# A recommendation tower on one core: first dense layer on two tiles at once, 36 cross terms for 40, an eleventh field by one-hot rows

## The reference

```python
e = jnp.stack([tbl_f[ids[:, f]] for f in range(26)], axis=1)      # 2048 x 26 x 32, tables of 1000 to 125000 rows
x1 = einsum('bik,bjk,hij->bhk', e, e, W1) + b1[None, :, None]     # 128 outputs
x2 = einsum('bik,bjk,hij->bhk', x1, e, W2) + b2[None, :, None]    # 128 outputs
z = jnp.sum(jnp.concatenate([x1, x2], axis=1), axis=-1)           # 2048 x 256
h = jnp.concatenate([z, dense_ctx], axis=1)                       # 2048 x 272
h = jnp.maximum(h @ W_top1 + b_top1, 0.0)                         # 512
h = jnp.maximum(h @ W_top2 + b_top2, 0.0)                         # 256
y = h @ W_top3
```

## Time and profile before

| | us |
|---|---|
| median of 3 runs | 509.12 |
| lowest, highest | 507.92, 512.33 |
| the profiled execution's own time | 510.54 |
| its span, first to last instruction | 508.7 |

### The profile page before, as it was taken

The page is one execution under the profiler, slowest core; times in us unless marked ns, Lnnn a source line. Parts: engine busy times, 40 slices in busy tenths (PEclk is TensorE's granted clock), DMA queues, the critical chain, the costliest instruction groups (busy, mean ns, idle before and its releaser), DMA issues.

```text
span 508.7 us, 25085 instructions
## 1 busy us (share of the span) xinstructions
PE 479.8 (94%) x10786; PEld 461.8 (91%) x10786; DVE 377.7 (74%) x1095; ACT 253.5 (50%) x530; POOL 348.9 (69%) x274
## 2 busy tenths in 40 slices
PE   4998889969699999999999999999999999999998
PEld 4887879869699999999999999999999999999997
DVE  8698949495778788797969597959695968773202
ACT  8866835364525463636364545454454545455111
POOL 5888977467887888787878787878787887700000
PEclk9999999989989999999999999999999999999999
DMA  6620022120111102020202020202020200000000
GB/s 216 171 95 13 15 56 47 28 60 13 37 40 30 44 16 53 13 59 10 59 12 58 13 58 13 57 13 59 11 59 12 59 10 12 9 1 3 1 1 1
DMA packets 14001, 19.57 MB, mean 38 GB/s; under 512 B 5123, under 2 KB 11528, under 8 KB 13838
## 3 DMA queue, kind: packets, MB, share of 16 engines
q0 software_dynamic: 8512, 4.38, 8.1%
q1 hardware_dynamic: 5454, 14.73, 8.0%
HBM read 19.08 MB, written 0.01 MB: 38 GB/s over the span
## 4 chain that ended last, share of the span: by engine, by line
PE 78%; DVE 8%; issue 3%; ACT 3%; DMA 3%; POOL 2%; SPq 1%; ACTq 0%; DVEq 0%; POOLq 0%
PE psum L927 21%; PE psum L901 18%; PE psum L946 12%; PE psum L972 8%; PE psum L880 7%; PE psum L994 4%; PE psum L922 4%; DVE work L631 3%; POOL emb L389 2%; DMA onehot<-in_tbl 2%; PE psum L967 2%; DVE onehot L479 2%; DMA emb<-in_tbl,idx 1%; ACT t_area L742 1%; ACT v L706 1%
## 5 line engine op out<-in xcount | busy, mean ns | idle before, releaser
L389 POOL DMA_INDIRECT emb<-in_tbl,idx x266 | 348.1, 1309 | 95.0 <-issue 63.5
L742 ACT COPY t_area<-psum 128x432 f32<-128x432 f32 x256 | 124.5, 543 | 98.2 <-PE psum L901 71.3
L631 DVE TENSOR_TENSOR work<-embT 128x32 f32<-128x32 f32 (+12 forms) x416 | 129.3, 386 | 0.0
L927 PE MATMUL psum<-t_area,v 128*128 (+1 forms) x1088 | 124.1, 275 | 0.0
L927 PEld LDWEIGHTS psum<-t_area,v 128*128 128x128 f32 x1088 | 122.8, 192 | 0.0
L901 PE MATMUL psum<-diag,work 64*64 64x54 f32 (+1 forms) x6144 | 102.1, 216 | 4.8 <-ACT t_area L742 2.0
L901 PEld LDWEIGHTS psum<-diag,work 64*64 64x64 f32 (+1 forms) x6144 | 93.3, 126 | 11.5 <-issue 6.0
L719 ACT COPY diag<-embT 32x416 f32<-32x416 f32 x128 | 69.9, 546 | 20.6 <-DVE embT L613 19.1
L946 PE MATMUL psum<-table_parts,onehot 125*128 125x96 bf16 x1350 | 63.7, 208 | 4.1 <-DVE onehot L479 2.4
L946 PEld LDWEIGHTS psum<-table_parts,onehot 125*128 125x128 bf16 x1350 | 59.4, 99 | 6.5 <-DVE onehot L479 2.7
L880 PE MATMUL psum<-diag,work 128*64 128x108 f32 (+1 forms) x1024 | 51.5, 262 | 8.5 <-DVE work L631 6.6
(11 more groups left out here) (96 smaller groups left out, 447.1 us busy)
## 6 DMA issues: line engine op xcount, KB each, us to landing
ids_all<-in_short_ids SPq DMA_DIRECT2D x15, 625.0 KB
emb<-in_tbl,idx POOLq DMA_INDIRECT x266
t_area<-in_L_rec_W SPq DMA_DIRECT2D x1, 1664.0 KB, 8.5
work<-in_W_top SPq DMA_DIRECT2D x2, 512.0 KB, 12.2
onehot<-in_tbl SPq DMA_DIRECT2D x5, 156.2 KB
onehot<-in_tbl SPq DMA_DIRECT2D x5, 125.0 KB
t_area<-in_L_rec_W SPq DMA_DIRECT2D x1, 338.0 KB, 4.0
idx<-in_ids SPq DMA_DIRECT2D x1, 208.0 KB, 2.5
```

The lines of the kernel that those rows point to most:

```text
L389: eng.indirect_dma_start(emb[n][:, f * K:(f + 1) * K], None, tables[f], bass.IndirectOffsetOnAxis(ap=idx[:, t * F + f:t * F + f + 1], axis=0),
L631: last = nc.vector.tensor_tensor(pairs[:, half, :, :, tri(r):tri(r) + r + 1], halves[:, g, :, 0:r + 1], halves[:, g, :, r:r + 1].broadcast ...
L742: nc.scalar.copy(dst, src).then_inc(t_out, 1)
L927: last = nc.tensor.matmul(z_ps(t)[:, NP:2 * NP], v[:, s, :], moments(slot), start=(a == 0), stop=(a == len(terms) - 1))
```

## The change

1. Layer 1 runs once for two tiles (a pair), with 256 columns in place of 128. It no longer stands inside a step. After every second step PE runs layer 2 of both tiles of the older pair and then layer 1 of the next pair (`layers`). The pair's hidden values take two PSUM banks, 4 and 7, and `h1_low` and `make_y` are done for two tiles at once, in every second tile of DVE.
2. The cross layer has 36 terms: 5 for x1 and 31 for x2. For this `pack` moves other pieces, in 10 copies where it had 7, with one wait of DVE for its own earlier copies.
3. 11 fields come by one-hot rows, in three parts of 4, 4 and 3 fields, before phases 1, 3 and 5. They take 38, 36 and 26 matmuls. Their PSUM banks are 7, 6 and 4. Parts 0 and 2 wait for `h1_low` of the pair, since they write where layer 1 wrote. So 15 gathers a tile remain.
4. The marks and the load of W_top3 move with this.

```diff
-FREE, U_Z2 = 5, U + 5
+FREE, U_Z2 = 8, U + 8
-U_Z1, N_Z1 = U + HF, 4
+U_Z1, N_Z1 = U + HF, 3
-SHORTS = 10
+SHORTS = 11
-PER_BANK = 5
+PER_BANK = 4
-MARK_PHASES = (0, 2, 3, 5, 6, 7)
+MARK_PHASES = (0, 2, 4, 6, 7)
...
         def rows_ps(part):
-            return psum[:, 7 - part, 0:PER_BANK * PARTS * K]
+            return psum[:, (7, 6, 4)[part], 0:PER_BANK * PARTS * K]
...
+        def h1_ps(half):
+            return psum[:, (4, 7)[half], :].rearrange("p (a b) -> p a b", b=2 * NP)
...
-                if not known or t >= 4:
-                    make_y(t - 4)
+                if n == 1 and (not known or t >= 5):
+                    for tile_of_pair in range(2):
+                        make_y(2 * i - 4 + tile_of_pair, tile_of_pair)
                 if not known or t >= 2:
                     pack(t - 1, 1 - n)
-                if not known or t >= 3:
-                    h1_low(t - 3)
+                if n == 1 and (not known or t >= 3):
+                    h1_low(i - 1)
...
-                        for part, at in enumerate((5, 6) if isinstance(t, int) and t == 1 else (2, 5)):
+                        for part, at in enumerate((5, 6, 7) if isinstance(t, int) and t == 1 else (1, 3, 5)):
...
-                    if part == 1 and not (isinstance(t, int) and t < 5):
-                        eng.wait_ge(y_ready, t - 3)
+                    if pair is not None:
+                        eng.wait_ge(y_ready if part == 1 else h1_lo_ready, 2 * pair + (1 if part == 1 else 3))
...
+            def layer1(pair):
+                if not (isinstance(pair, int) and pair == TILES // 2 - 1):
+                    eng.wait_ge(rows_ready, 2 * pair + 3)
+                eng.wait_ge(h1_lo_ready, 2 * pair + 1)
+                eng.wait_ge(z_out, 2 * pair + 2)
...
+                    if a == 2:
+                        eng.wait_ge(y_ready, 2 * pair + 1)
...
+                        if a == 0 and z is z_lo:
+                            eng.wait_ge(z_lo_ready, 2 * pair + 2)
...
+            def step(t, pair, n):
+                for half in range(2):
+                    t_units(t, half, pair)
+                if not isinstance(t, int) or t >= 2:
+                    cin(t - 1, n)
+            def layers(pair):
+                for n in range(2):
+                    layer2(2 * pair + n, pair, n)
+                layer1(pair + 1)
...
+            layer1(0)
             with eng.Fori(0, (LOOP[1] - LOOP[0]) // 2) as i:
                 with eng.Fori(0, 2) as n:
-                    step(2 * i + n + LOOP[0], n)
+                    step(2 * i + n + LOOP[0], i, n)
+                layers(i)
```

More of the change, by code:

```diff
@@ L298, in build @@
                 moves = [(0, hi - lo, 0, LOW, LOW * c, V_LOW + HF * (1 - c) + lo)]
[L299 to L303, removed]
+                for first, end, quadrant, _, slot in OTHERS[c]:
+                    a, z = max(lo, first), min(hi, end)
+                    if a < z:
+                        moves.append((a - lo, z - a, LOW, CONST + 1, 32 * quadrant, slot + a - first))
                 v_jobs.append(([("other", c, nu, CONST + 1) for nu in range(lo, hi)], moves))
@@ L323, in marks_in @@
         def marks_in(t):
-            layers, cross = t >= 3, t != 1
-            return len(MARK_PHASES) + 2 + 2 * layers + len(MARK_TERMS) * cross
+            layer1, layer2, cross = t >= 2 and t % 2 == 0, t >= 4 and t % 2 == 0, t != 1
+            return len(MARK_PHASES) + len(ROW_PARTS) + 2 * layer1 + 2 * layer2 + len(MARK_TERMS) * cross
         block = ctx.enter_context(nc.Block())
@@ L751, in z_move, with h1_move @@
                     .then_inc(z_out, 1)
[L753 to L759, removed]
+            def h1_move(pair):
+                if not (isinstance(pair, int) and pair < 1):
+                    eng.wait_ge(h2_full, 2 * pair)
+                for half in range(2):
+                    eng.wait_ge(h1_full, 2 * pair + half + 1)
+                    nc.scalar.activation(h1_hi[:, 2 * half:2 * half + 2, :], h1_ps(half), ACT.Relu).then_inc(h1_out, 1)
             def step(t, i, n):
@@ L777, in step @@
                 if not known or t >= 1:
-                    z_move(t - 1, 1 - n)
+                    z_move(t - 1, i - 1 + n, 1 - n)
+                if n == 0 and (not known or t >= 2):
+                    h1_move(i - 1)
             eng.wait_ge(consts_ready, 1)
@@ L792, in _ @@
                 step(t, t // 2, t % 2)
[L793 to L796, removed]
+            z_move(TILES - 1, TILES // 2 - 1, 1)
+            h1_move(TILES // 2 - 1)
         @block.tensor
@@ L848, in make_v, with t_units @@
                     last.then_inc(prep_full, 1)
-            def t_units(t, half):
+            def t_units(t, half, pair):
                 eng.wait_ge(pairs_ready, 2 * t + half + 1)
@@ L931, in cin, with short_rows @@
                 last.then_inc(z_full, 1)
-            def short_rows(t, part):
+            def short_rows(t, part, pair):
                 eng.wait_ge(onehot_ready, t)
@@ L964, in layer1 @@
                 for a in range(N1 // NP):
-                    dst = h1_ps(t)[:, a, :]
+                    if a == 2:
+                        eng.wait_ge(y_ready, 2 * pair + 1)
+                    dst = h1_ps(a // 2)[:, a % 2, :]
                     cols = slice(a * NP, (a + 1) * NP)
-                    nc.tensor.matmul(dst, top1d[:, cols], denseT[:, bass.ts(t, NP)], start=True, stop=False)
+                    nc.tensor.matmul(dst, top1d[:, cols], denseT[:, bass.ts(pair, 2 * NP)], start=True, stop=False)
@@ L993, in layer2 @@
                     for s in range(N1 // NP):
-                        last = nc.tensor.matmul(dst, h1[:, s * NP:(s + 1) * NP], top2[:, s, :], start=False,
-                                                stop=(h1 is lo and s == N1 // NP - 1))
-                        if h1 is lo and s == N1 // NP - 2:
+                        last = nc.tensor.matmul(dst, h1[:, s, n * NP:(n + 1) * NP], top2[:, s, :], start=False,
+                                                stop=(h1 is h1_lo and s == N1 // NP - 1))
@@ L997, in layer2 @@
+                        if h1 is h1_lo and s == N1 // NP - 2:
                             last.then_inc(progress, 1)
                 last.then_inc(h2_full, 1)
-            def step(t, n):
-                known = isinstance(t, int)
-                t_units(t, 0)
-                if not known or t >= 3:
-                    layer1(t - 3, n)
-                t_units(t, 1)
-                if not known or t >= 3:
-                    layer2(t - 3)
-                if not known or t >= 2:
+            def step(t, pair, n):
+                for half in range(2):
+                    t_units(t, half, pair)
+                if not isinstance(t, int) or t >= 2:
```

137 lines of the change are left out of this document (60 added, 77 removed).

## The result

| | us |
|---|---|
| median after (542.29 to 546.06) | 543.11 |
| median before, same chip (507.92 to 512.87) | 510.73 |
| after / before | 1.0648, 95% interval 1.0573 to 1.0723 |
| the profiled execution's own time; its span | 546.06; 544.1 |

The change makes the kernel 6.5% slower. The forecast was 530.0, range 515 to 540: right in sign and in what the loss comes from, a circle through DVE and the gathers, 13 too low, and 3 outside its range. The profiled execution is 3 over the median, where the forecast had allowed 1.4.

The account below looks back on a forecast made before the run. PE bounds the kernel before, a two-step circle through DVE after. A pair: 55.45 + 1.9 gathers + 0.3 clock = 57.65; five pairs +24.7, start +2.6, tail -6.4, total +20.9: 530.0 for the median, range 515 to 540.

Parts of the forecast that it names:

- a circle over two steps: PE's part 0 waits for DVE's `h1_low`, DVE's next tile for PE: 55.45 a pair, before 52.7.
- The pieces of the circle behind the transpose: DVE's work up to `h1_low`, done 24.45 after even R, with pack 4.0; then part 0 to next R, 8.75.
- The late gathers: DVE's second transpose of the odd tile waits for POOL's last gather, 0.3 to 3.4 late; 1.9 a pair taken.
- The long gather: On POOL, a gather beginning well inside DVE's pairs lasts until they end: 3.43 and 4.06 for 0.94.
- The clock: Half clock on PE after its waits, mostly falling into layer 1: 0.3 a pair, between 0 and 1.7.
- The start: R (end of a step's short rows) of step 4 at 182.1 for 179.5: +2.6, within 3 either way.
- Where PE waits: PE waits 5 us from even R, part inside layer 1 for `z_low`, the rest before part 0.
- The tail: After R of step 14 no one-hot is left on DVE, so PE's work decides: -6.4.
- Rival 1: On POOL, no late gathers: a pair is 55.75 and the time 520.5; chance 0.24.
- Rival 2: On PE, the half clock hits the short rows in each pair: +1.4 x 5, 537; chance 0.12.
- Rival 3: PE stays the bound and part 0 doesn't wait: ten steps 243.5, time 483; chance 0.06.

Follow-up runs that it names:

- ahead2: The changed kernel with the gathers' marks moved four marks earlier (AHEAD 2 for 6), nothing else: 512.48 us, 1.001 of before.
- h1_first: The changed kernel with `h1_low` moved ahead of the pack in DVE's odd tiles, nothing else: 542.07 us, 1.061 of before.
- swap_banks: The changed kernel with short-row parts 0 and 1 trading PSUM banks, so part 0 waits for `make_y` alone: 540.86 us, 1.060 of before.
- z_early: The changed kernel with `z_low` and `make_y` ahead of the second pairs in odd tiles, `h1_low` still last: 546.18 us, 1.070 of before.
- all_four: The changed kernel with `h1_low` before the pack, `z_low` and `make_y` early, AHEAD 2, parts before phases 3, 4, 5: 484.91 us, 0.950 of before.

## Why the prediction was right in kind and too low

- **The bound moves from PE to a circle over two steps: right.** Even step to odd step takes 37.1 in the mean for 35.4; odd to even 22.5 for 22.25.
- **The pieces of the circle behind the transpose: right.** From its start to `z_low` done it takes 15.0 to 15.5 (329.66 - 314.63), from there to `h1_low` done 6.0 to 6.7, from part 0 to R 9.0 for 8.75. The pack took 3.5 to 3.7 in odd tiles and 4.1 in even ones, for 4.0. Layer 1 at full clock takes 3.32 for 28 matmuls in the after trace (499.75 to 503.07), 0.119 each: 256 columns cost what 128 do, as the trace before had it.
- **The late gathers: this step failed in size.** "I take 1.9, the middle" over R + 2.9 makes R + 4.8 for the second transpose. It began at R + 7.77, 6.73, 6.85, 6.80 and 4.29, in the mean 6.5. The missing 1.7, five times, is 8.4 of the 10.0 that the ten steps took more (298.2 for 288.2). In the stretch shown the miss is three parts: the first gather began at R + 2.4 and not 1.6; both long gathers occurred, 5.7 in place of the middle's 4.5, and so in four of five pairs; slightly long ones came to 1.25 for 0.8. Together 2.45, the 26.86 at which the last began less the middle of 22.9 to 25.9. It even lies past the upper end (25.9). The middle between two patterns was no pattern at all. The fifth pair, with one long gather in that stretch, came out at 35.0. What the prediction took for granted here, that POOL cannot start the 15 before the stretch, is the marks' doing: ahead2 takes it away, a pair is 5.3 shorter and the kernel 30.6 faster. That is more than the 3.6 of lateness in the mean, since both transposes also start earlier than R + 2.9.
- **The long gather: read too simply.** "One that begins well inside the pairs lasts until they end" holds for some gathers only. In the trace before, two gathers begin 1.27 after the start of a run of pairs; one (185.37) takes 3.88, the other (212.43) 1.12. After the change two begin 1.63 after it and take 3.51 (291.51) and 1.04 (411.01). Even the same gather, the 60th of the program, is held in one execution and not in another. The first row is the changed kernel, 1.83 after the start of a run of pairs; the second is h1_first, whose list is the same up to there, 1.85 after it:

```profile
105.59 3.31 POOL L394 DMA_INDIRECT emb<-in_tbl,idx  x1 [0.30 <-issue]
```

```profile
105.04 1.20 POOL L394 DMA_INDIRECT emb<-in_tbl,idx  x1 [0.30 <-issue]
```

  What decides is not known, so the count of one or two long ones was what had been seen, and no rule. The Trainium skill was also read too simply there: the same section (SBUF — State Buffer, Who interferes with whom) says that a `tensor_tensor` with both inputs in SBUF contends with what GpSimd reads from SBUF. The pairs have both inputs in SBUF, and the list `idx` of the gathers lies there too. No run here tells whether that read is what is held.
- **The clock: near.** Layer 1 after `z_low` takes 4.6 to 5.3 at the 1.2 GHz level. In the loop most of it lies beside make_y and the pack; DVE waits 3.4 in five pairs for the hidden values, 0.7 a pair for the 0.3 taken. In the first pair less lies beside it: PE waits 7.97 until 146.47, the second `h1_low` waits 1.50 for the hidden values, and is done at 153.10 where I had 151 (159.9 less 8.75).
- **The start: past its bound in this execution.** R of step 4 is 186.7 for 182.1, 4.6 later where I had allowed 3. Of the 4.6 about 2.0 is the late `h1_low`, 2.0 lies between it and R of step 3, where PE has gaps of 0.57 and 0.90, and 0.6 in the step behind. Not all of it belongs to the kernel. h1_first and swap_banks run the same order up to `z_low` of the first pair, and in their profiles the second transpose ahead of it waits 2.5 and 2.3 for its gather, where it waits 5.9 in the changed kernel. Why it does is not shown. `z_low` comes 2.35 and 1.8 earlier and R of step 4 is 183.7 and 183.5, inside the bound.
- **Where PE waits: wrong.** The forecast put 5 "part of it inside layer 1 for `z_low` ..., the rest before part 0". Measured, 6.2 a pair inside layer 1 and under 0.4 before part 0. I had `z_low` due at R + 18 without the late gathers, and layer 1 at full clock behind it. In the pair shown `z_low` is done at R + 21.9 (329.66), and layer 1 then takes 4.6, so that PE comes to part 0 just before `h1_low` is ready. The way from the transpose to `h1_low` lasts no longer than I had summed, but the wait stands elsewhere. For the sum it makes little difference, for a remedy a great deal: h1_first and swap_banks mend the place named in the forecast and give next to nothing.
- **The tail: right**, 59.2 after R of step 14 for 59.3.
- **The rivals.** Rival 1 (no late gathers) is the reverse of what happened. The Trainium skill (SBUF — State Buffer, Who interferes with whom) was on its side: by it a `tensor_tensor` leaves descriptor generation alone. The trace after disagrees again for the two that took 3.51 and 4.10, where most take 0.94. Rival 2 (half clock on the short rows) didn't happen: part 0 took 1.79 each time. Its mechanism is real, as z_early shows, where the wait stands directly ahead of the rows; here layer 1 took the blow. Rival 3 (PE stays the bound) is what all_four reaches, by another order of the same work.
- **The range** ended at 540, which is 530.0 with both terms at their upper ends (1.5 x 5 for the gathers, 3 for the start). In the profiled execution both went past these: 3.6 for the gathers in the mean over 3.4 (25.9 less 22.6 is 3.3, in fact), 4.6 for the start over 3. Its time is 14.7 over the 531.4 forecast for it: 10.0 from the ten steps, 4.6 from the start. The bound on the gathers was no bound, since it took the first gather's start as known.

What stays open: how the rest of the 4.6 before step 4 divides between clock and gaps; what makes one gather long and another short; and what the merged layer 1 or the eleventh field cost or give each by itself, since no run has one without the other.

## What to carry to other kernels

Where a change makes PE wait on a helper engine, write the circle: each piece from the moment PE frees it to the moment PE needs it again, the DMA issue queue included; if one stretch of it becomes shorter than that queue's work, the queue is part of the circle, and both its long cases should be counted, not their middle. Two waits in a row on the same engine can stand in for one another: here taking away either gave nothing (540.9, 546.2), both together 29. And a change that loses 6% as written was a gain of 5% with three calls moved, gathers freed earlier and two parts of the short rows put later, so find the wait that took its place before the change is dropped.

## What was not expected of the hardware

- A gather that begins inside a run of `TENSOR_TENSOR` may last until 0.8 to 1.1 after the run's end, before and after (3.43 and 4.06 in the earlier trace rows; 3.51 and 4.10 above), for 0.94 alone. Not every one does: where it begins in the run doesn't decide it (3.51 and 1.04 at the same 1.63), nor does which gather it is (3.31 and 1.20 above). The difference of one shifted a whole pair by about 2.5 (R + 4.3 for R + 6.8).
- After waits of 4 to 8 in layer 1 the granted clock in the trace after was 0.50 for 6.8 in three pairs and for 10.2 in the other three, and which of the two did not follow from the wait before it in any plain way: layer 1 took 5.27 after 6.76 of wait in one pair and 4.60 after 6.43 in another. A wait of 1.73 ahead of part 0 in ahead2 was also followed by half clock (2.86 for 1.79), as three of its five were (waits of 1.82, 1.82 and 1.73); the other two (1.74 and 1.73) were not.
